# Attention block with routed experts: the last batch from its last projection to the routed rows in two halves of two tiles

## The chip, the cores and the metric

One core of a Trainium2 chip. The metric is the device time of the whole program in microseconds, the median of the runs; lower is better. Engines are called by their short names: PE (TensorE, matmuls), DVE (VectorE), ACT (ScalarE), POOL (GpSimd) and SP (SyncE, which issues DMAs here). Each runs its own queue in order and waits on semaphores.

## The reference

Four batches of 512 tokens with 256 features pass through one block.

```python
mod = (silu(c) @ wmod).reshape(4, 6, 1, -1)          # sa, ca, ga, sb, cb, gb
ga = sign(ga) * max(abs(ga), 0.25);  gb likewise
h = layernorm(x) * (1 + ca) + sa
x = x + ga * attention(h)       # 16 heads of 128, rms norm of q and k, rope factors,
                                # scores capped by 50 tanh(s / 50), causal softmax, @ wo.T
h = layernorm(x) * (1 + cb) + sb
x = x + gb * (experts(h) + shared(h))
# experts: logits = h @ gate.T; softmax over 64; the best 3 of 8 groups, of these the best 6 experts;
# each token goes to slot flat * 96 + min(pos, 95); per expert silu(g) * u, times Wd; the six results
# are weighted and summed.  shared: silu(h @ Sg.T) * (h @ Su.T) @ Sd.T, width 352
```

Routing is sequential in the tokens: `pos`, the place of a token in its expert's buffer, counts all tokens before it.

## The kernel before

A batch is four tiles of 128 tokens (`TT` = 4). The attention runs in periods, one per head: in period `p` PE does the scores of head `p`, the transposes and the projection of head `p - 1`, the projections q, k, v of head `p + 2`, and the product of head `p`. The routing of batch `b` is laid over periods 1 to 15 of batch `b + 1`, a piece per period, and its 24 table writes (one indirect DMA for each tile and each of the six choices, `table`, L510 to L514) over periods 9 to 15 of POOL, as `SPREAD` says (L64). The last batch has no such cover. In its place stands the shared expert: `shared_up(j)` (L1391) is one third of a batch's first layer, so there are twelve, j = 0 to 11; ACT takes silu (`shared_silu`), DVE multiplies (`shared_mul`), PE multiplies by the second layer after every third (`shared_down(b)`, L1460), and DVE adds that to x (`shared_half`, `shared_res`). After that PE goes through the 64 experts.

The order of all this is written out by hand, engine by engine. For the last batch it reads, after the last period:

- PE (L1456 to L1497): `o_t` transposes the last head's output; `proj` multiplies it by the head's rows of `wo`; `shared_up(2)` and `(3)`; `h2_t` transposes the normed rows; half of `shared_down(0)`; `router` gives the logits; the other half; `shared_up(4)`; `positions`, which adds up the chosen experts over the tokens; `shared_up(5)`, `(6)`, `shared_down(1)`; a transpose of `lastp`, the last token of each expert; the rest of the shared work.
- DVE (L1145 to L1185): `wo_low`, `out_low` (the low part of the split operands), `x_most` adds fifteen heads, times the gate, to x; `x_last` does so with the last head; `ln_stats`, `h2_scaled`, `h2_modulated` make the normed rows in `pay`; then `route_soft`, `route_groups`, `route_experts`, `route_counts`, `route_slots`, and for each tile `route_tile`, after which POOL may write that tile's six tables.
- ACT (L707 to L717): the high parts of the operands, silu of groups 0 to 3, `h2_static` (copy of the transposed rows), `route_exp`, silu of the rest.
- POOL (L551 to L562): `ln_rstd`, the tables of tiles 0 and 1, the gather of the last tokens' rows (it needs `lastp`), the tables of tiles 2 and 3.
- SP (L410 to L431): weights of experts, the normed rows to memory, and, when all table writes have landed, the rows of the first eight experts.

PSUM has eight banks. Banks 0 to 3 hold the shared expert's first layer, 4 and 5 the projection (`yps`) and later `shared_down`; 6 and 7 the last batch's transposed rows, and 6 its logits and positions (`sbank`, L324).

Of the kernel before, what the change touches and what calls it, by code (L numbers as in the profile page):

```python
# [28 lines left out]
P = 128  # L29
# [11 lines left out]
C = 96  # L41
# [22 lines left out]
SPREAD = {9: (0, 3), 10: (3, 4), 11: (7, 4), 12: (11, 1), 13: (12, 4), 14: (16, 4), 15: (20, 4)}  # L64


def build(nc, x, wqkv, wo, qkw, cossin, ct, wmod, gate, sgu, sd, wgu, wd, out):
    with ExitStack() as ctx:
# [175 lines left out]
        def wd_place(v):  # L244
# [27 lines left out]
            wcol_rdy x_shared o95_g cmb_ps cmb cmb2 outd""".split()  # L272
# [6 lines left out]
        acc2_in = [sem(f"acc2_in{b}") for b in range(B)]  # L279
# [43 lines left out]

        def sbank(b):  # L324

            return 6 if is_last(b) else SB
# [3 lines left out]
        def _(sp):  # L330
# [86 lines left out]
            sp.wait_ge(s["h2s_rdy"], B)  # L417
# [19 lines left out]
            def third_sum():  # L437

                sp.wait_ge(ys[2], adds(2, E))
                for b in range(B):  # L440
                    sp.dma_start(accs[2][:, b * TT:(b + 1) * TT], acc_d[2][b * T:(b + 1) * T].rearrange("(i p) d -> p i d", p=P)).then_inc(acc2_in[b], 16)
# [21 lines left out]
        def _(pool):  # L463
# [22 lines left out]
            def ln_rstd(l):  # L486

                pool.wait_ge(s["aggr"], TT * (l + 1))
                pool.tensor_scalar(rstd[:], mv[:, :, 1], 1e-5, None, ALU.add).then_inc(s["var_eps"], 1)
                pool.wait_ge(s["var_eps"], l + 1)  # L490
                pool.tensor_tensor(rstd[:], rstd[:], neghalf[:, 0:TT], ALU.pow).then_inc(s["rstd_rdy"], 1)

# [58 lines left out]
            ln_rstd(ln2(B - 1))  # L551
            for i in range(TT // 2):
# [7 lines left out]
            for i in range(TT // 2, TT):  # L560
# [15 lines left out]
        def _(a):  # L576
# [49 lines left out]

            def wo_high(b, n):

                if some(cnt(b, n - 1)):
                    a.wait_ge(s["y_rdy"], 2 * cnt(b, n - 1))  # L630
                act_(woh[:], wos[:, bass.ds(head(n), 1), :].squeeze(1), ACT.Copy).then_inc(s["woh_rdy"], 1)
# [10 lines left out]
            def h2_static(b):  # L642

                a.wait_ge(s["xt_ps"], ln2(b) + 1)
                act_(h2s, ps[:, sbank(b):sbank(b) + KC, :], ACT.Copy).then_inc(s["h2s_rdy"], 1)

            def route_exp(b):

                a.wait_ge(s["soft"], b + 1)
                for i in range(TT):  # L650
                    ins = act_(lg[:, i, :], ps[:, sbank(b), i * E:(i + 1) * E], ACT.Exp, bias=mx[:, i:i + 1], accum_out=rs[:, i:i + 1])
# [131 lines left out]
        def _(v):  # L783
# [92 lines left out]

            def wo_low(b, n):
# [37 lines left out]

            def e3(ap, n):
                return ap.unsqueeze(2).to_broadcast([P, TT, n])

            def max8(b, v8, src, keep):

                for i in range(TT):
                    step(b, nc.vector.max(v8[:, i, :], src[:, i, :]), i == TT - 1)
                step(b, nc.vector.memset(v8[:, :, keep:8], -1.0))

            def taken(b, c, out, v8, src):

                for i in range(TT):
                    step(b, nc.vector.match_replace(out[:, i, :], v8[:, i, :], src[:, i, :], -1.0), i == TT - 1)

            def route_soft(b):  # L930
                rt[0] = 0
                v.wait_ge(s["logit_ps"], b + 1)
                nc.vector.tensor_reduce(mx, ps[:, sbank(b), 0:TT * E].rearrange("p (i e) -> p i e", i=TT), X, ALU.max, negate=True).then_inc(s["soft"], 1)

            def route_groups(b):

                v.wait_ge(s["rt_exp"], b + 1)
                step(b, nc.vector.tensor_reduce(gsc.rearrange("p i n -> p (i n)"), lg.rearrange("p i (n c) -> p (i n) c", n=NG), X, ALU.max))
                step(b, nc.vector.reciprocal(rs, rs), False)
                max8(b, g8, gsc, TG)  # L940
                taken(b, 4, gm, g8, gsc)
                step(b, nc.vector.scalar_tensor_tensor(out=tmp.rearrange("p i (n c) -> p (i n) c", n=NG),
                                                       in0=gm.rearrange("p i n -> p (i n)").unsqueeze(2).to_broadcast([P, TT * NG, GS]), scalar=0.0,
                                                       in1=lg.rearrange("p i (n c) -> p (i n) c", n=NG), op0=ALU.is_lt, op1=ALU.mult))

            def route_experts(b):

                max8(b, w8, tmp, K)
                taken(b, 5, left, w8, tmp)
                ts(selr[:], left, 0.0, None, ALU.is_lt).then_inc(s["sel_rdy"], 1)  # L950

            def route_counts(b):

                for i in range(TT):
                    step(b, nc.vector.max_index(ei[:, i, :], w8[:, i, :], tmp[:, i, :]), i == TT - 1)
                step(b, cp(pay[:, :, D + K:TOK], ei[:, :, 0:K]))
                step(b, tt(pay[:, :, D:D + K], w8[:, :, 0:K], e3(rs, K), ALU.mult), False)
                step(b, cp(pay[:, :, TOK].bitcast(I32), iotat[:, bass.ds(b * TT, TT)]), False)

            def route_slots(b):  # L960

                v.wait_ge(s["sel_rdy"], b + 1)
                v.wait_ge(s["pos_rdy"], b + 1)
                posv = ps[:, sbank(b), 0:TT * E].rearrange("p (i e) -> p i e", e=E)
                step(b, ts(over, posv, float(C - 1), SKIP, ALU.is_ge, ALU.mult))
                tt(slotm, posv, iota96[:].unsqueeze(1).to_broadcast([P, TT, E]), ALU.add).then_inc(s["pos_used"], 1)
                v.wait_ge(s["pos_used"], b + 1)
                step(b, tt(slotm, over, slotm, ALU.add))
# [17 lines left out]
            def route_last(b):  # L986
# [4 lines left out]
                step(b, nc.vector.tensor_reduce(count, sel.rearrange("p i e -> p e i"), X, ALU.add))  # L991
                step(b, tt(carr[:], carr[:].bitcast(F32), count, ALU.add))
# [12 lines left out]
            def rows_clamped():  # L1005
# [5 lines left out]
                                               op0=ALU.add, op1=ALU.mult).then_inc(s["mrow_rdy"], 1)  # L1011

            def period(b, p):
# [35 lines left out]
                if not (is_last(b) and isinstance(p, int) and p >= H - 2):  # L1049
                    squares_sum(b, p + 2)  # L1050
                if some(cnt(b, p - 1)):
                    y_add(b, p - 1)
                o_norm(b, p)
                if is_last(b) and isinstance(p, int) and p == H - 1:
                    shared_mul(0)
# [53 lines left out]
            def x_most(b):  # L1109

                v.wait_ge(s["y_added"], 2 * cnt(b, H - 2))
                xb = xs[:, b * TT:(b + 1) * TT, :]
                v.wait_ge(s["rows_in"], 16 * (b + 2))
                tt(yacc, yacc, rcur[:, 0:1, :].to_broadcast([P, TT, D]), ALU.mult).then_inc(s["x2_rdy"], 1)
                v.wait_ge(s["x2_rdy"], 2 * b + 1)
# [482 lines left out]
```

## Time and profile before

| what | us |
|---|---|
| median of 3 runs | 1039.97 |
| lowest, highest | 1035.8, 1043.36 |
| profiled execution, its own time | 1048.57 |
| its span, first to last instruction | 1046.7 |
| PE busy in the span | 982.6 (94%) |
| DVE busy | 680.4 (65%) |
| ACT busy | 586.1 (56%) |
| POOL busy | 382.6 (37%) |

The time line of the page cuts the span in 40 slices; a digit is the busy share in tenths.

```profile
PE   4999999999999999999999999999989789999992
PEld 4799999999999999999999999999955356566661
DVE  3566657768778876868887696788568133222366
ACT  2566766676666667666766666666541024433430
POOL 2222222223223554312354532235523615455660
PEclk9899999999999999999999999999999899999985
DMA  9992000001000101100010011100361049999747
```

One slice is 26 us. Attention fills the first 29 slices, up to about 770 us; the last batch's routing and the shared expert lie in slices 30 to 32, the experts from there to about 1010 us, and the rest adds the sums to x and writes it out. PEclk is the clock that PE was granted, in tenths of full speed: the higher of two levels, 2.4 GHz, is full, the lower is 1.2 GHz.

### The profile page before, as it was taken

How to read it: one execution, taken by the hardware profiler on the slowest of the kernel's cores; microseconds unless marked ns; L12 is line 12 of the kernel's file. 1: busy time of each engine (PE TensorE's matmuls, PEld its weight loads, DVE VectorE, ACT ScalarE, POOL GpSimd, SP SyncE). 2: the span in 40 equal slices, each digit the busy share in tenths (PEclk: the TensorE clock that was granted, in tenths of full speed). 3: DMA queues.
4: the chain of work that ended last, by engine and by line, in shares of the span. 5: the costliest groups of instructions: out<-in, count | busy, mean ns of one | idle time of the engine just before them, and what ended most of it. 6: DMA issues, size and time to landing. Idle time of an engine off the chain costs nothing.

```text
span 1046.7 us, 18148 instructions
## 1 busy us (share of the span) xinstructions
PE 982.6 (94%) x6301; PEld 874.1 (84%) x6301; DVE 680.4 (65%) x1775; ACT 586.1 (56%) x1093; POOL 382.6 (37%) x454
## 2 busy tenths in 40 slices
PE   4999999999999999999999999999989789999992
PEld 4799999999999999999999999999955356566661
DVE  3566657768778876868887696788568133222366
ACT  2566766676666667666766666666541024433430
POOL 2222222223223554312354532235523615455660
PEclk9899999999999999999999999999999899999985
DMA  9992000001000101100010011100361049999747
GB/s 348 335 348 90 0 0 1 1 2 56 2 1 18 43 33 38 36 22 1 13 46 28 24 37 60 49 3 15 99 180 57 17 118 303 300 292 298 164 74 240
DMA packets 67037, 99.22 MB, mean 95 GB/s; under 512 B 10157, under 2 KB 48176, under 8 KB 66574
## 3 DMA queue, kind: packets, MB, share of 16 engines
q1 hardware_dynamic: 41678, 70.43, 20.8%
q0 software_dynamic: 11808, 12.87, 6.2%
q10 hardware_dynamic: 13472, 14.90, 4.9%
q8 instruction: 46, 0.75, 0.3%
q14 instruction: 33, 0.27, 0.1%
HBM read 66.03 MB, written 38.78 MB: 100 GB/s over the span
## 4 chain that ended last, share of the span: by engine, by line
PE 79%; DVE 12%; issue 3%; ACT 2%; DMA 2%; POOL 1%; SPq 0%; POOLq 0%; DVEq 0%
PE ps L1308 22%; PE ps L1361 12%; PE ps L1334 11%; PE ps L1349 7%; PE ps L1514 7%; PE ps L1529 5%; PE ps L1398 3%; PE ps L1341 2%; PE ps L1317 2%; PE ps L1320 2%; PE ps L1507 1%; PE ps L1467 1%; PE ps L1521 1%; ACT prob L615 1%; DVE arena L975 1%
## 5 line engine op out<-in xcount | busy, mean ns | idle before, releaser
L615 ACT ACTIVATE prob<-ps,rn 128x512 f32<-128x512 f32 (+3 forms) x256 | 121.1, 526 | 122.3 <-PE ps L1334 115.4
L1308 PE MATMUL ps<-wh,hth 128*128 128x384 f32 x512 | 178.6, 349 | 5.7 <-DVE htl L814 3.6
L1308 PE MATMUL ps<-wh,htl 128*128 128x384 f32 x512 | 173.0, 338 | 0.0
L1308 PE MATMUL ps<-wl,hth 128*128 128x384 f32 x512 | 172.9, 338 | 0.0
L859 DVE TENSOR_REDUCE ss<-arena 128x8 f32<-128x1024 f32 x64 | 78.0, 1219 | 128.0 <-ACT arena L591 127.8
L1361 PE MATMUL ps<-vx,prob 128*128 128x129 f32 (+1 forms) x1280 | 153.4, 274 | 0.2 <-POOL prob L507 0.2
L1361 PEld LDWEIGHTS ps<-vx,prob 128*128 128x128 f32 x1280 | 148.2, 191 | 0.5 <-POOL prob L507 0.5
L591 ACT ACTIVATE arena<-ps 128x1024 f32<-128x1024 f32 x64 | 65.7, 1026 | 123.2 <-PE ps L1308 123.2
L504 POOL TENSOR_SCALAR_AFFINE_SELECT prob<-prob 128x384 f32<-128x384 f32 x64 | 35.4, 554 | 256.4 <-ACT prob L621 256.4
L570 POOL DMA_INDIRECT acc<-wos,arena x64 | 94.0, 1468 | 92.9 <-ACT wos L735 68.9
L513 POOL DMA_INDIRECT slot_rows<-pay,arena x96 | 99.4, 1035 | 43.2 <-issue 24.7
L498 POOL TENSOR_TENSOR rn<-rtmp,neghalf 128x8 f32<-128x8 f32 x64 | 105.3, 1645 | 5.3
L1308 PEld LDWEIGHTS ps<-wh,hth 128*128 128x128 f32 x512 | 97.6, 191 | 7.1 <-DVE htl L814 4.0
L1308 PEld LDWEIGHTS ps<-wl,hth 128*128 128x128 f32 x512 | 97.6, 191 | 0.0
L1308 PEld LDWEIGHTS ps<-wh,htl 128*128 128x128 f32 x512 | 97.2, 190 | 0.0
L1334 PE MATMUL ps<-qth,kth 128*128 128x512 f32 (+3 forms) x256 | 87.7, 342 | 6.4 <-DVE arena L889 4.0
L496 POOL TENSOR_SCALAR rtmp<-ss 128x8 f32<-128x8 f32 x64 | 12.5, 195 | 217.8 <-DVE ss L859 217.5
L1199 DVE TENSOR_TENSOR xn<-ps,arena 96x176 f32<-96x176 f32 x64 | 21.6, 337 | 104.0 <-ACT arena L726 80.5
L621 ACT ACTIVATE prob<-prob 128x1280 f32<-128x1280 f32 x64 | 83.7, 1308 | 0.0
L1334 PE MATMUL ps<-qtl,kth 128*128 128x512 f32 (+3 forms) x256 | 82.6, 323 | 0.0
L1334 PE MATMUL ps<-qth,ktl 128*128 128x512 f32 (+3 forms) x256 | 82.5, 322 | 0.0
L889 DVE TENSOR_TENSOR arena<-ps,arena 128x512 f32<-128x512 f32 x118 | 75.6, 681 | 3.5 <-PE ps L1349 3.4
(206 smaller groups left out, 2214.5 us busy)
## 6 DMA issues: line engine op xcount, KB each, us to landing
wge<-in_wgu SPq DMA_DIRECT2D x20, 352.0 KB
slot_rows<-pay SPq DMA_DIRECT2D x1, 6456.0 KB, 33.8
acc<-pay SPq DMA_DIRECT2D x3, 2048.0 KB, 18.1
arena<-slot_rows ACTq DMA_DIRECT2D x56, 100.9 KB
warena<-in_wqkv SPq DMA_DIRECT2D x1, 4992.0 KB, 20.8
arena<-in_wgu SPq DMA_DIRECT2D x14, 352.0 KB
warena<-acc SPq DMA_DIRECT2D x8, 512.0 KB, 6.9
late_t<-in_wd ACTq DMA_DIRECT2D x14, 192.0 KB
```

The source lines that it names most:

```text
L498: pool.tensor_tensor(rn[:, bass.ds(head(n), 1), :].squeeze(1), rtmp[:], neghalf[:], ALU.pow).then_inc(s["r_rdy"], 1)
L513: pool.indirect_dma_start(buf_d, bass.IndirectOffsetOnAxis(ap=sloti[:, i * K + k:i * K + k + 1], axis=0), pay[:, i, :], None, bounds_check ...
L570: pool.indirect_dma_start(acc_d[acc_of(e)], bass.IndirectOffsetOnAxis(ap=tokc[:, e % TR:e % TR + 1], axis=0), orow[e % ORING], None, bound ...
L615: act_(prob[:, OFF[j]:OFF[j] + w], sflat[:, OFF[j]:OFF[j] + w], ACT.Tanh, scale=rn[:, bass.ds(head(n), 1), TT + j:TT + j + 1].squeeze(1)). ...
L621: act_(prob[:, 0:1280], prob[:, 0:1280], ACT.Exp, scale=CAP).then_inc(s["expd"], 1)
L859: nc.vector.tensor_reduce(ss[:].rearrange("p (c i) -> p i c", c=2), sq, X, ALU.add).then_inc(s["ss_rdy"], 1)
L889: tt(ya, yp, ya, ALU.add).then_inc(s["y_added"], 1)
L1308: last = mm(ps[:, i, 0:3 * DH], hp[:, k, i * P:(i + 1) * P], wp[:, k, :], start=(k == 0 and m == 0), stop=(k == KC - 1 and m == 2))
L1334: last = mm(sflat[:, OFF[j]:OFF[j] + w], kp[:, j * P:(j + 1) * P], qp[:, T - w:T], start=(m == 0), stop=(m == 2))
L1349: last = mm(yps[:, i, :], op[:, i * P:(i + 1) * P], wp[:], start=(m == 0), stop=(m == 2))
L1361: last = mm(o, prob[:, c:c + P], vx[:, bass.ds((vslot(n) * TT + j) * (DH + 1), DH + 1)], start=(j == 0), stop=(j == i))
L1514: last = mm(ps[0:C, 1 + e % 2, 0:2 * M], xgt[:, e % 2, k, :], wgus[e % RING][:, k, :], start=(k == 0), stop=(k == KC - 1))
```

## The change

From the last head's projection on, the last batch's chain is cut into two halves of two tiles (`TH` = 2).

- The gate row is multiplied into the last head's rows of `wo` once, at period 12 (`wo_gate`), so the last projection comes out gated, and `x_last(q)` is one addition from PSUM. The sum of the other heads is gated inside the last period (`y_gated`).
- Transposed output, low parts, projection, x, statistics, rstd, modulation, transposes, copy, logits, exps and each routing step exist once for each half. The counts of the second half's positions include the first half's chosen experts.
- Banks: the halves of the last output go to 7 and 6, the transposed rows to 6 and 7, logits and positions of half q to bank 4 + q, `shared_down` to 6 and 7.
- PE's order: half of `shared_up(2)` stands before the last projection, half after it; `shared_up(3)` between the halves' routers; `shared_down(0)` in one piece after the first half's positions.
- POOL: three tiles' tables before the gather, one after it; `SPREAD` moves two writes from period 15 to period 12.
- The last batch no longer adds its counts to `carr`; the final loads of two accumulators use one semaphore with the third and wait until the third is scaled (`cmb2`).

```diff
-SPREAD = {9: (0, 3), 10: (3, 4), 11: (7, 4), 12: (11, 1), 13: (12, 4), 14: (16, 4), 15: (20, 4)}
+SPREAD = {9: (0, 3), 10: (3, 4), 11: (7, 4), 12: (11, 3), 13: (14, 4), 14: (18, 4), 15: (22, 2)}
+TH = TT // 2
...
+            sp.wait_ge(s["cmb2"], B)
             for a in range(2):
                 sp.wait_ge(ys[a], adds(a, E))
...
-            ln_rstd(ln2(B - 1))
-            for i in range(TT // 2):
+            ln_rstd_half(0)
+            ln_rstd_half(1)
+            for i in range(TT - 1):
...
-            out_t(B - 1, H - 1)
+            out_t_half(0)
+            out_t_half(1)
             shared_silu(2)
-            shared_silu(3)
             act_(warm[:], neghalf[:, 0:1], ACT.Exp)
-            h2_static(B - 1)
-            route_exp(B - 1)
-            for j in range(4, 3 * B):
+            h2_half(0)
+            route_exp_half(0)
+            h2_half(1)
+            route_exp_half(1)
+            for j in range(3, 3 * B):
...
+            def x_last(q):
+
+                v.wait_ge(s["y_rdy"], 2 * cnt(B - 1, H - 1) + (q - 1))
+                v.wait_ge(s["x2_rdy"], 2 * B + q)
+                xb = xs[:, (B - 1) * TT + q * TH:(B - 1) * TT + (q + 1) * TH, :]
+                tt(xb, xb, yps[:, q * TH:(q + 1) * TH, :], ALU.add).then_inc(s["y_added"], 1)
...
+            shared_mul(0)
+            x_most(0)
+            out_low_half(0)
+            out_low_half(1)
+            x_most(1)
+            x_last(0)
+            last_stats(0)
+            last_scaled(0)
+            x_last(1)
+            last_modulated(0)
             shared_mul(1)
...
+            route_slots(b, HALF[1])
+            route_tile(b, 2)
+            route_tile(b, 3)
             shared_half(0, 0)
...
+            shared_half(0, 1)
             shared_mul(5)
...
+            shared_up(2, (0,))
+            pe.wait_ge(s["y_added"], 2 * cnt(B - 1, H - 2))
+            pe.wait_ge(s["wol_rdy"], B * H)
+            last_proj(0)
+            last_proj(1)
+            shared_up(2, (1,))
+            h2_t_half(0)
+            router_half(0)
             shared_up(3)
...
+            h2_t_half(1)
+            router_half(1)
+            shared_up(4)
+            positions_half(0)
             pe.wait_ge(s["ld_sd"], 32)
...
+            shared_down(0)
             shared_up(5)
+            positions_half(1)
             shared_up(6)
             shared_down(1)
+            shared_up(7)
```

PE's queue before, from the end of the last projection to the second `shared_down` (L1398 is `shared_up`, L1467 `shared_down`, L1289 the transposes of the normed rows, L1378 the router, L1384 to L1387 the positions):

```order
L1398 MATMUL ps<-warena 96x512 x4
L1398 MATMUL ps<-warena 128x512 x4
L1289 MATMUL ps<-ident,pay 128x128 x8
L1467 MATMUL ps<-wos,warena 128x256 x6
L1378 MATMUL ps<-gates,arena 128x64 x8
L1467 MATMUL ps<-wos,warena 128x256 x6
L1398 MATMUL ps<-warena 128x512 x4
L1384 MATMUL ps<-selr,trir 128x256
```

The same place in the changed kernel (L1524 is `shared_up`, L1495 the transposes of a half, L1502 the router of a half, L1509 the first matmul of a half's positions):

```order
L1524 MATMUL ps<-warena 96x512 x2
L1495 MATMUL ps<-ident,pay 128x128 x4
L1502 MATMUL ps<-gates,arena 128x64 x4
L1524 MATMUL ps<-warena 128x512 x4
L1495 MATMUL ps<-ident,pay 128x128 x4
L1502 MATMUL ps<-gates,arena 128x64 x4
L1524 MATMUL ps<-warena 128x512 x4
L1509 MATMUL ps<-selr,trir 128x128
```

Ahead of the transposes stand two matmuls of `shared_up` where eight stood, and between transposes and router nothing where six of `shared_down` stood.

DVE's queue before, around the tiles of the routing (L978 ends a tile, L906 is `shared_mul`, here j = 5, L1132 and L1138 are `shared_half` and `shared_res`):

```order
L978 CAST arena<-arena 128x6
L906 TENSOR_TENSOR warena<-ps,warena 96x512
L1132 TENSOR_TENSOR warena<-ps,rgb 128x512
L1138 TENSOR_TENSOR xs<-xs,warena 128x1024
L975 SCALAR_TENSOR_TENSOR arena<-iotae,pay,arena 128x64 x6
```

In the changed kernel (L1021 to L1024 are `route_slots` of the second half, L1031 and L1034 a tile, L1218 `shared_half`, L943 `shared_mul`):

```order
L1021 TENSOR_SCALAR arena<-ps 128x128
L1022 TENSOR_TENSOR arena<-ps,iota 128x128
L1024 TENSOR_TENSOR arena<-arena 128x128
L1031 SCALAR_TENSOR_TENSOR arena<-iotae,pay,arena 128x64 x6
L1034 CAST arena<-arena 128x6
L1031 SCALAR_TENSOR_TENSOR arena<-iotae,pay,arena 128x64 x6
L1034 CAST arena<-arena 128x6
L1218 TENSOR_TENSOR warena<-ps,rgb 128x512 x2
L943 TENSOR_TENSOR warena<-ps,warena 96x512
```

`shared_mul(5)`, which stood after the second tile, now stands after the fourth and after both halves of `shared_down(0)`.

## Rows read from the trace of the kernel before

**Rows 1.** Windows: stretch, us, busy and count by engine, PEclk, DMA share, GB/s.
```profile
770.00:785.00 15.00, 12.32 (x42) 7.12 (x43) 12.34 (x25) 4.25 (x6) 1.64 (x2) 0.89 0.72 211
```

**Rows 2.** Timeline of PE: start, us, instruction, [idle before <-releaser].
```profile
765.13 2.40 PE L1361 MATMUL ps<-vx,prob 128*128 128x129 f32 x20
769.22 0.66 PE L1341 MATMUL ps<-ident,arena 128*128 128x128 f32 x4 [1.69 <-DVE arena L897]
771.67 0.36 PE L1349 MATMUL ps<-woh,oth 128*128 128x256 f32 x1 [1.79 <-DVE otl L875]
...
773.69 8.14 PE L1398 MATMUL ps<-warena 128*96 128x512 f32 x16
782.84 1.06 PE L1289 MATMUL ps<-ident,pay 128*128 128x128 f32 x8 [1.01 <-DVE pay L844]
```

**Rows 3.** Timeline of DVE, the hand-over.
```profile
770.88 0.69 DVE L875 TENSOR_TENSOR otl<-ps,oth 128x512 fp32r<-128x512 f32 x1 [0.78 <-ACT oth L625]
771.49 1.22 DVE L1114 TENSOR_TENSOR arena<-arena,rcur 128x1024 f32<-128x1024 f32 x1
...
774.48 1.21 DVE L1123 TENSOR_TENSOR arena<-ps,rcur 128x1024 f32<-128x1024 f32 x1
...
776.99 1.41 DVE L789 BATCH_NORM_STATS2 bst<-xs 128x6 f32<-128x256 f32 x4
...
781.04 1.66 DVE L844 SCALAR_TENSOR_TENSOR pay<-xn,rstd,rcur 128x256 f32<-128x256 f32 x4
```

**Rows 4.** Timeline of POOL, last LayerNorm and table writes.
```profile
778.90 0.51 POOL L489 TENSOR_SCALAR rstd<-mv 128x4 f32<-128x4 f32 x1 [9.60 <-DVE mv L792]
779.50 1.13 POOL L491 TENSOR_TENSOR rstd<-rstd,neghalf 128x4 f32<-128x4 f32 x1
799.12 1.09 POOL L513 DMA_INDIRECT slot_rows<-pay,arena  x1 [18.50 <-DVE arena L978]
...
815.52 1.00 POOL L558 DMA_INDIRECT lrow<-h_rows,lidx  x1 [0.30 <-issue]
...
830.92 0.97 POOL L513 DMA_INDIRECT slot_rows<-pay,arena  x1 [0.30 <-issue]
```

**Rows 5.** Timeline of PE, routing and shared matmuls.
```profile
798.98 3.70 PE L1398 MATMUL ps<-warena 128*128 128x512 f32 x8 [0.39 <-DVE warena L906]
...
808.43 0.30 PE L1488 MATMUL ps<-ident,arena 128*64 128x128 f32 x1 [0.56 <-DVE arena L990]
808.57 10.47 PE L1398 MATMUL ps<-warena 128*128 128x512 f32 x24
...
824.28 1.88 PE L1398 MATMUL ps<-warena 128*128 128x512 f32 x4
...
835.90 6.07 PE L1398 MATMUL ps<-warena 128*96 128x512 f32 x8 [1.10 <-issue]
843.38 5.46 PE L1467 MATMUL ps<-wos,warena 128*128 128x256 f32 x24 [1.41 <-DVE warena L906]
849.63 0.39 PE L1507 MATMUL ps<-ident,arena 96*128 96x96 f32 x2 [0.79 <-DVE warena L1132]
```

**Rows 6.** Timeline of ACT: copy of the transposed rows; silu of group 9.
```profile
783.94 1.02 ACT L645 ACTIVATE arena<-ps 128x1024 f32<-128x1024 f32 x1
...
832.40 0.60 ACT L705 ACTIVATE warena<-ps 128x512 f32<-128x512 f32 x1 [14.20 <-remote]
```

**Rows 7.** Lines of DVE, 785 to 812, by form: busy us, mean ns.
```profile
L975 DVE SCALAR_TENSOR_TENSOR arena<-iotae,pay,arena 128x64 f32<-128x64 f32 x24 | 5.3, 282 | 0.0
L1132 DVE TENSOR_TENSOR warena<-ps,rgb 128x512 f32<-128x512 f32 x4 | 2.7, 685 | 3.2 <-PE ps L1467 3.2
```

**Rows 8.** Timeline of SP: first rows of experts; first final load.
```profile
833.03 0.28 SPq L429 DMA_DIRECT2D arena<-slot_rows  x1
...
1020.82 0.36 SPq L454 DMA_DIRECT2D warena<-acc  x1
```

**Rows 9.** Timeline of DVE: scaling of the third sum's last quarter.
```profile
1014.20 1.21 DVE L1214 TENSOR_TENSOR warena<-warena,rgb 128x1024 f32<-128x1024 f32 x1
```

More of the change, by code:

```diff
@@ L914, in step @@
                     v.wait_ge(s["rt"], STEPS * b + rt[0])
+            ALL = (0, TT)
+            HALF = [(q * TH, (q + 1) * TH) for q in range(2)]
             def e3(ap, n):
[L917 to L928, printed above, removed]
@@ L946, in route_experts @@
[L946 to L958, printed above, removed]
@@ L960, in route_slots @@
[L960 to L968, printed above, removed]
+                return ap.unsqueeze(2).to_broadcast([P, ap.shape[1], n])
@@ new lines, in routed, with nth, max8 @@
+            def routed(b, r, c):
+                bank = 4 + r[0] // TH if is_last(b) else SB
+                n = r[1] - r[0]
+                return ps[:, bank, c * n * E:(c + 1) * n * E].rearrange("p (i e) -> p i e", e=E)
+            def nth(b, r):
+                return b + 1 + r[0] // TH
+            def max8(b, v8, src, keep, r):
+                for i in range(*r):
+                    step(b, nc.vector.max(v8[:, i, :], src[:, i, :]), i == r[1] - 1)
+                step(b, nc.vector.memset(v8[:, r[0]:r[1], keep:8], -1.0))
@@ new lines, in route_experts, with route_counts @@
+            def route_experts(b, r=ALL):
+                sl = slice(*r)
+                max8(b, w8, tmp, K, r)
+                taken(b, left, w8, tmp, r)
+                ts(selr[:, sl, :], left[:, sl, :], 0.0, None, ALU.is_lt).then_inc(s["sel_rdy"], 1)
+            def route_counts(b, r=ALL):
+                sl = slice(*r)
+                for i in range(*r):
+                    step(b, nc.vector.max_index(ei[:, i, :], w8[:, i, :], tmp[:, i, :]), i == r[1] - 1)
+                step(b, cp(pay[:, sl, D + K:TOK], ei[:, sl, 0:K]))
+                step(b, tt(pay[:, sl, D:D + K], w8[:, sl, 0:K], e3(rs[:, sl], K), ALU.mult), False)
+                if r[0] == 0:
+                    step(b, cp(pay[:, :, TOK].bitcast(I32), iotat[:, bass.ds(b * TT, TT)]), False)
@@ new lines, in route_slots @@
+            def route_slots(b, r=ALL):
+                sl, n = slice(*r), r[1] - r[0]
+                v.wait_ge(s["sel_rdy"], nth(b, r))
+                v.wait_ge(s["pos_rdy"], nth(b, r))
+                posv = routed(b, r, 1 if is_last(b) else 0)
+                step(b, ts(over[:, sl, :], posv, float(C - 1), SKIP, ALU.is_ge, ALU.mult))
+                tt(slotm[:, sl, :], posv, iota96[:].unsqueeze(1).to_broadcast([P, n, E]), ALU.add).then_inc(s["pos_used"], 1)
+                v.wait_ge(s["pos_used"], nth(b, r))
+                step(b, tt(slotm[:, sl, :], over[:, sl, :], slotm[:, sl, :], ALU.add))
@@ L1371, in h2_t @@
                 pe.wait_ge(s["hmod"], 2 * b + 2)
[L1372 removed]
+                xn_t(pay, SB)
             def router(b):
@@ L1392, in shared_up @@
+            def shared_up(j, us=(0, 1)):
                 b, m = j // 3, j % 3
@@ new lines, in _ @@
+            pe.wait_ge(s["o_normed"], 2 * B * H)
+            for i in range(TT):
+                last = pe.transpose(ps[:, 7 - i // TH, i * P:(i + 1) * P], on[:, i, :], ident[:])
+            last.then_inc(s["ot_ps"], 1)
+            shared_up(2, (0,))
[6 more added lines that the diff above has]
+            router_half(0)
```

237 lines of the change are left out of this document (148 added, 89 removed).

## The prediction

> **What bounds the kernel now.** I read the page first, then its chain of waits, then the order of time around the change. TensorE (PE) is busy in nearly every slice and makes most of the chain, so a gain must shorten PE's path. The change touches one place: the stretch between the last head's attention and the first expert. In its first 15 us the clock is 0.89 [rows 1]. Three things are to be seen there.
>
> First, the hand-over. PE ends the last head's product at 767.5, waits 1.69 and 1.79 us for VectorE (DVE) and ScalarE (ACT), projects, then has two of the `shared_up` groups as cover, and still waits 1.01 us at 782.84 for the modulated rows [rows 2]. DVE is the reason: after the split of the last transpose it does a product of 1024 columns and an addition of the same size before it looks at the last projection, and the same pair after it [rows 3]. Second, routing on DVE, then 24 table writes on GpSimd (POOL) from 799.12, one in about 1.3 us, with a gather at 815.52 among them; the last starts at 830.92 [rows 4]. SyncE can fetch the experts' rows at 833.03 [rows 8]. Third, PE does shared matmuls all the while and reaches the first expert at 849.63 [rows 5]. Rows were fetched long before: from 833.03 on, so **PE's own queue, not the routed rows, is the path**.
>
> **The stall.** Group 10 of `shared_up` should take what the groups before it took: 24 matmuls in 10.47 us are three groups, 3.45 each. It starts at 824.28, group 11 not before 835.90, and the last `shared_down` at 843.38 [rows 5]. That is 19.1 us where two groups and the row's own wait of 1.41 are 8.3: **10.8 us too long**. ACT shows the same: the silu of group 9, whose matmuls are recorded as ended by 819.04, runs at 832.40, half a microsecond after POOL's last table write ends (831.9) [rows 4 to 6]. PE works without a gap until 824 and then trickles, as if completions were held back from about the gather on.
>
> **The change part by part, on PE's path.** Times of the new kernel are counted on the old one's axis from 769.22, where the last transposes start in both.
>
> *Taken away.* (a) The 1.79 us ahead of the last projection: half of group 2 now stands there (1.7 us of matmuls; transposes end at 769.85, the half at 771.6, the first half of `otl` is ready at about 771.2). (b) The slow clock: 0.89 over 15 us is 3.3 us at the lower of the two levels, 1.65 us lost [rows 1]; it began in the second of two gaps near each other, and one of them is now filled. (c) The 1.01 us before the transposes of the rows. (d) 0.39 ahead of group 6 and 0.56 ahead of the transpose of the last positions [rows 5]. Together 5.4.
>
> *Brought in.* (e) PE projects until 773.0, does the other half of group 2 until 774.7, and then has nothing until the first half of the rows. That half: the projection's first half ends at 772.5; `x_last` is one 512-column step, 0.7 [rows 7]; statistics half of 1.41, 0.7; aggregates 0.2; POOL's two steps 1.8 (from its start at 778.90 to 780.63, and 0.1 to be started); modulation half of 1.66, 0.83; 0.14 to PE: 776.9 [rows 3, 4]. PE waits 2.2. (f) ACT's copy of each half stood behind a `shared_down` half before; now the router half follows at once. The copy of 1024 columns took 1.02 [rows 6], one of 512 about 0.6: 0.65 twice, 1.3. (g) `shared_down(1)` waits for `shared_mul(5)`, which DVE now does behind four more steps. PE: 776.9, transposes, copy and router half 2.15, group 3 to 782.5, second half to 784.65, group 4 to 788.1, positions 788.55, `shared_down(0)` 5.3 to 793.85, group 5 to 797.3, positions 797.9, group 6 to 801.35. DVE: slots of the second half 0.95 from 797.95, two tiles of 1.5 each (six of L975 and a cast [rows 7]), two 512-column steps 1.3, the product 0.65: 803.85. PE waits 2.5. (h) Group 9 waits about 0.3 for `shared_mul(7)`, now behind `shared_add(1)` after a later transpose. Together 6.3, and three more small position matmuls, 0.1.
>
> So without the stall **PE's path is longer by 1.0 us**, not shorter. Gate folding removes two 1024-column steps of DVE behind the projection [rows 3] and adds one of 256 columns at period 12, where PE is the bound; it is already in (e). The moved tables (3, 4, 4, 2 in place of 1, 4, 4, 4 at periods 12 to 15) cost nothing: four in a period are hidden now by a period of about 11 us. The final loads now also wait for the third sum's scaling, which starts at 1014.20 and runs 1.22, while SyncE gets there at 1020.82 [rows 8, 9]: 5.4 us of cover. The weights 15 to 17 are asked for about 4 us earlier, with nobody waiting.
>
> *The stall again.* POOL: first tile's slots at 788.6 + 0.95 + 1.5 = 791.05, the first write 0.8 later, 791.9 in place of 799.12: 7.2 us earlier. The same 25 starts end at about 824.7 in place of 831.9 [rows 4]. By (g), PE ends `shared_down(2)` at about 825.4 and only then starts group 10. If the hold ends with POOL's last write, it ends before PE would trip over it, and all 10.8 go. If it doesn't depend on POOL, none goes. Those are the bounds; the nearest row, ACT's start 0.5 us after POOL's end, speaks for the first.
>
> **The sum.** Against the profiled execution (1048.57, of which 1046.7 are its span): 1048.57 - 10.8 + 1.0 = 1038.8. The three timed runs, 1035.8 to 1043.36 with a median of 1039.97, lie 5 to 13 us below the profiled one. Without its stall the profiled one would be 1037.8, inside them. So I take it that the timed median holds about 2.2 us of such a stall: 1039.97 - 2.2 + 1.0 = **1038.8**.
>
> A rule against halving is in the Trainium skill, "VectorE: DVE Perf Modes", on the errata mechanism: one large tile pays the memory latency once, many small ones pay it each time. The trace agrees: a 1024-column step takes 1.22 and one of 512 takes 0.69 [rows 3, 7], so a split costs about 0.16. Some twenty steps are split, 3 us more on DVE, of which only what stands in (g) reaches PE.
>
> **Rivals.**
> Main case, 0.42: as above, 1038.8, by itself 1035 to 1042.
> A, 0.20: the stall is as large in the timed runs, and they are quicker than the profiled one for another reason. For: it is in ACT's and PE's rows alike. Against: the profiled run is 8.6 above the median, and that is nearly its size. 1039.97 - 10.8 + 1.0 = 1030.2.
> B, 0.16: the timed runs have none of it, the change then only lengthens PE's path: 1041.0. The Trainium skill has such a mechanism, "NOTIFIC — the notification-queue block", section "Overflow: three behaviours, one of which stalls the engine": records of the profile that back up can throttle an engine. No run here shows it yet.
> C, 0.17, slower: the clock. It fell in the old kernel at the gap of 1.79 that followed one of 1.69 [rows 1, 2]. The new gaps of 2.2 with 0.65 behind a short transpose group, and of 2.5, are as large; if both bring a fall of the size seen, that is 2 x 1.65, and with the stall's share unchanged 1039.97 + 1.0 + 3.3 = 1044.3. It decides from a gap of about 1.8 us that has another near it; against it, the single 1.69 and 1.41 are not followed by one.
> D, 0.05: the halves wait on each other longer than I see, or the rows come after PE (about 829 against 839.8 by my count), 1046 and more.
>
> **The numbers.** Low 1029 takes in A, high 1045 takes in C. Less than 1% can't be told from no change here, that is 10.4 us, 1029.6 to 1050.4. Faster by over 1% is the lower part of A and a little luck with the first half, 0.12; slower by over 1% the tail of D, 0.04; within, 0.84.
>
> **What would show it.** (a) No idle time at the last projection, and a clock of 1.0 in the 15 us after 770; if it is below, C. (e) An idle time near 2.2 before the first transposes of four. (g) One near 2.5 at the second `shared_down`. POOL's first table write of the batch near 792. For the stall: group 10 as one block, ACT's silu of group 9 right after its matmuls, the first expert's transpose at 839 to 841. If the trickle is there again at full length, the sum against the profiled execution is wrong by up to 10.8 us; if the path is clean and the timed runs fall to 1030, the share of the stall in the median was wrong.

## The result

| | median, us | runs |
|---|---|---|
| before | 1037.87 | 20, 1035.8 to 1043.36 |
| changed | 1042.09 | 20, 1038.34 to 1045.69 |

Changed to before: 1.0036, 95% interval 1.0026 to 1.0046. The change makes the kernel **slower by 4 us**, where the forecast was 1.2 us faster (1038.8 against 1039.97). Two later groups of runs gave 1.0038 (1.0025 to 1.0050) and 1.0039 (1.0026 to 1.0053). The profiled execution of the changed kernel took 1043.18 us, 1041.4 of them its span.

### The profile page after: what moved, and what is told of

It is laid out like the page before. It is cut to its first block, busy times and chain, and to the rows that moved or that the text cites. A ratio compares the mean times of both kernels' runs of the same rounds, so it can differ in the third digit from the quotient of the medians.

```text
span 1041.4 us, 18174 instructions
## 1 busy us (share of the span) xinstructions
PE 977.2 (94%) x6304; PEld 873.3 (84%) x6304; DVE 681.2 (65%) x1788; ACT 587.0 (56%) x1095; POOL 384.2 (37%) x456
## 4 chain that ended last, share of the span: by engine, by line
PE 75%; DVE 11%; DMA 7%; ACT 3%; issue 3%; POOL 1%; SPq 0%; ACTq 0%; POOLq 0%; DVEq 0%
PE ps L1406 22%; PE ps L1459 12%; PE ps L1432 11%; PE ps L1447 7%; DMA acc<-wos,arena 6%; PE ps L1653 4%; PE ps L1524 3%; PE ps L1668 3%; PE ps L1415 2%; PE ps L1590 2%; PE ps L1418 2%; PE ps L1439 2%; ACT prob L621 1%; DMA warena<-in_wqkv 1%; DVE bst L816 1%
```

## The profile after

The timeline of PE in the changed kernel; its first row answers to the transposes of [rows 2], its last to the first expert's of [rows 5]. L1524 is `shared_up`, L1590 `shared_down`, L1495 the transposes of the rows, L1502 the router.

```profile
769.16 0.66 PE L1604 MATMUL ps<-ident,arena 128*128 128x128 f32 x4 [1.18 <-DVE arena L935]
769.76 1.96 PE L1524 MATMUL ps<-warena 128*96 128x512 f32 x4
...
776.86 0.66 PE L1495 MATMUL ps<-ident,pay 128*128 128x128 f32 x4 [2.01 <-DVE pay L1111]
778.20 1.10 PE L1502 MATMUL ps<-gates,arena 128*128 128x64 f32 x8 [0.69 <-ACT arena L670]
...
782.63 0.60 PE L1495 MATMUL ps<-ident,pay 128*128 128x128 f32 x4
783.91 1.10 PE L1502 MATMUL ps<-gates,arena 128*128 128x64 f32 x8 [0.69 <-ACT arena L670]
...
788.60 5.44 PE L1590 MATMUL ps<-wos,warena 128*128 128x256 f32 x24
...
803.93 6.97 PE L1590 MATMUL ps<-wos,warena 128*128 128x256 f32 x24 [2.47 <-DVE warena L943]
...
818.36 3.67 PE L1524 MATMUL ps<-warena 128*128 128x512 f32 x8 [0.47 <-DVE warena L943]
821.86 5.36 PE L1590 MATMUL ps<-wos,warena 128*128 128x256 f32 x24
827.06 7.03 PE L1524 MATMUL ps<-warena 128*128 128x512 f32 x16
835.49 5.46 PE L1590 MATMUL ps<-wos,warena 128*128 128x256 f32 x24 [1.41 <-DVE warena L943]
841.74 0.39 PE L1646 MATMUL ps<-ident,arena 96*128 96x96 f32 x2 [0.78 <-DVE warena L1218]
```

The waits stand where they were counted: none at the projection, 2.01 for the first half of the rows (2.2 forecast), 0.69 twice for ACT's copies (0.65), 2.47 at the second `shared_down` (2.5), 0.47 at group 9 (0.3). What was not in the sum is in the second column: the second `shared_down` takes 6.97 us, the first 5.44 and the third 5.36 for the same 24 matmuls. Groups 10 and 11 (of `shared_up`) are one block of 7.03 us, so this execution has no stall.

DVE, POOL, ACT and SyncE of the same execution, answering to [rows 3], [rows 4], [rows 6] and [rows 8]. The DVE row is the modulation of the first half:

```profile
775.92 0.88 DVE L1111 SCALAR_TENSOR_TENSOR pay<-xn,rstd,rcur 128x256 f32<-128x256 f32 x2 [0.19 <-DVE xs L1086]
```

```profile
792.17 1.06 POOL L518 DMA_INDIRECT slot_rows<-pay,arena  x1 [12.34 <-DVE arena L1034]
...
825.22 0.98 POOL L518 DMA_INDIRECT slot_rows<-pay,arena  x1 [0.30 <-issue]
```

```profile
822.06 0.60 ACT L730 ACTIVATE warena<-ps 128x512 f32<-128x512 f32 x1 [3.55 <-PE ps L1524]
```

```profile
827.33 0.28 SPq L425 DMA_DIRECT2D arena<-slot_rows  x1
```

The first half's rows leave DVE at 776.8, POOL's tables start at 792.17 (791.9 forecast) and end 5.7 us earlier than in [rows 4]; the silu of group 9 follows its matmuls; the rows are fetched 14 us before PE needs them. All this is early for nobody: PE's queue is the path.

The windows of the same execution. The columns are those of [rows 1]; the seventh, behind POOL's, is the granted clock.

```profile
770.00:785.00 15.00, 11.62 (x53) 6.76 (x52) 11.04 (x35) 4.48 (x11) 2.63 (x4) 1.00 0.72 213
...
801.00:811.00 10.00, 7.53 (x27) 5.93 (x26) 7.10 (x22) 0.60 (x1) 7.96 (x7) 0.83 0.03 2
```

At the hand-over the clock is 1.00 in this execution where it was 0.89 [rows 1] (two later profiles of the same kernel, below, have 0.89 again); behind the 2.47 us wait it is 0.83 over 10 us, 3.4 us at the lower level (1.2 GHz). That is where `shared_down` lost 1.5 to 1.6 us.

## The experiments

**Path** below is the time from the last head's transposes to the first expert's transpose, on PE, in one profiled execution: 849.63 - 769.22 - 10.8 = 69.6 before, 841.74 - 769.16 = 72.6 after. Ratios are to the kernel before in the same group of runs, which share a chip. The ratio is worked out from all runs and not from the two medians. There were three groups, with the kernel before at 1046.55, 1038.13 and 1037.79 us. The changed kernel itself was not run in group 1, so a forecast "below the changed kernel" can be read in groups 2 and 3 only.

| run | group | path | falls of the clock on it | median | ratio (95%) |
|---|---|---|---|---|---|
| e1_mul5_early | 1 | 76.0 | 1 | 1047.14 | 0.9998 (0.9978 to 1.0017) |
| e2_dummy | 1 | 79.0 | 2 | 1045.46 | 0.9984 (0.9968 to 1.0001) |
| e3_fill | 1 | 75.1 | 1 | 1043.05 | 0.9956 (0.9939 to 0.9973) |
| e4_all | 1 | 72.6 | 1 | 1038.35 | 0.9910 (0.9889 to 0.9931) |
| before_again | 2 | 69.4 | 1 | 1036.99 | one execution |
| after_again | 2 | 74.4 | 2 | 1042.28 | 1.0038 (1.0025 to 1.0050) |
| e6_gate | 2 | 68.8 | 1 | 1034.58 | 0.9972 (0.9957 to 0.9986) |
| e4_again | 2 | 64.5 | 0 | 1031.44 | 0.9935 (0.9912 to 0.9957) |
| f1_warm2 | 3 | 71.0 | 0 | 1038.33 | 1.0003 (0.9992 to 1.0015) |
| e1_again | 3 | 70.0 | 1 | 1037.23 | 0.9996 (0.9984 to 1.0008) |
| e3_again | 3 | 68.0 | 0 | 1036.21 | 0.9977 (0.9961 to 0.9993) |
| after_third | 3 | 74.4 | 2 | 1042.39 | 1.0039 (1.0026 to 1.0053) |

### The two kernels again

> The kernel before, once more, for its profile beside the others of this call. Theory 1 (the 10.8 us for which group 10 of shared_up trickled was a rare event): no such stretch, the first transpose of the experts starts at 838 to 839. Theory 2 (completions of TensorE are held back while POOL writes its tables, in many executions and by a length that varies): a stretch of 3 to 13 us between 800 and 832 in which group 8's or 9's silu starts late after its matmuls, ended within 3 us of POOL's last table write.

> The changed kernel, timed on the same chip as the experiments. Theory 1 (the change costs 3.7 us by TensorE's waits and clock, whatever the chip): 0.3 to 0.5% above the kernel before. Theory 2 (the held completions are part of the timed runs on a chip where the kernel before takes 1046 instead of 1038 us, and the change, which lets POOL start 7 us earlier, moves or loses them): the ratio differs from 1.0036, either 0.5% or more below 1 (the stall gone, as the forecast's case A had it) or above 1.006.

> The changed kernel, beside its three variants on one chip. Theory (TensorE's waits and the slow clock in them): 0.3 to 0.5% above the kernel before, with one or two falls of the clock between 775 and 812. Rival (if this is the chip of the first call, where late completions cost every kernel 7 to 9 us): within 0.2% of the kernel before.

PE of before_again, and its window over the hand-over:

```profile
773.51 8.74 PE L1398 MATMUL ps<-warena 128*96 128x512 f32 x16
782.17 1.06 PE L1289 MATMUL ps<-ident,pay 128*128 128x128 f32 x8
...
823.42 7.03 PE L1398 MATMUL ps<-warena 128*128 128x512 f32 x16
...
838.10 0.38 PE L1507 MATMUL ps<-ident,arena 96*128 96x96 f32 x2 [0.79 <-DVE warena L1132]
```

```profile
770.00:777.00 7.00, 6.18 (x17) 3.94 (x18) 6.77 (x9) 0.00 (x0) 0.00 (x0) 0.51 0.79 224
```

No stall, and the first transpose of the experts at 838.1, as theory 1 had it: group 10 is in one block, and the whole execution takes 1036.99. The clock falls at the hand-over, longer than in the first profile (0.51 over 7 us), and there it costs next to nothing: the slow matmuls end when the rows come, 782.2, and the wait of 1.01 [rows 2] is gone instead. The rows come 13.5 us after the last transposes where they came 13.6 us after them in the first profile.

The changed kernel's second profile:

```profile
776.05 0.66 PE L1495 MATMUL ps<-ident,pay 128*128 128x128 f32 x4 [2.00 <-DVE pay L1111]
777.39 1.10 PE L1502 MATMUL ps<-gates,arena 128*128 128x64 f32 x8 [0.69 <-ACT arena L670]
...
784.81 1.10 PE L1502 MATMUL ps<-gates,arena 128*128 128x64 f32 x8 [0.69 <-ACT arena L670]
...
804.81 7.14 PE L1590 MATMUL ps<-wos,warena 128*128 128x256 f32 x24 [2.46 <-DVE warena L943]
```

```profile
770.00:785.00 15.00, 11.62 (x45) 6.18 (x43) 10.24 (x33) 3.97 (x9) 2.63 (x4) 0.89 0.66 191
777.00:785.00 8.00, 6.92 (x22) 3.62 (x22) 4.37 (x19) 1.64 (x6) 1.31 (x2) 0.79 0.34 117
801.00:811.00 10.00, 7.54 (x25) 5.44 (x24) 7.95 (x29) 0.60 (x1) 7.87 (x8) 0.83 0.03 2
```

And the windows of its third profile, after_third:

```profile
777.00:785.00 8.00, 6.94 (x22) 3.43 (x20) 4.87 (x21) 1.64 (x6) 1.31 (x2) 0.79 0.38 131
801.00:811.00 10.00, 7.55 (x24) 5.26 (x23) 8.45 (x33) 0.60 (x1) 7.87 (x8) 0.83 0.03 2
```

The waits are the same to 0.01 us, but the clock fell **twice**. From one router half to the other it takes 7.42 us where the first profile has 5.71: 1.7 us for the fall at 777 to 785, which the first profile did not have. The third profile has both falls too. Over the 15 us from 770 on these two have 0.89, as much slow clock as the kernel before had [rows 1]: it only stands behind another wait. So the path is 74.4 in two of three, and against 69.5 before that is 4.9 us more, in the first 3.1; the medians differ by 4.2, 4.2 and 4.6.

### Throwaway work in the waits

e2_dummy:

```diff
             shared_up(6)
+            for _ in range(5):
+                mm(ps[:, 4, D:2 * D], ident[:], sds[:, 0, :], start=True, stop=True)
             shared_down(1)
```

> The changed kernel, with ten throwaway passes (five fp32 products of 128x128 by 128x256 of a constant, some 2.1 us) that TensorE does in its wait before the second round of down projections; nothing reads them. The wait itself stays. Theory (the clock fell because TensorE was idle for those 2.47 us, and shared_down(1) took 6.97 us instead of 5.4 for it): the granted clock stays at 1.0 in this stretch, shared_down(1) takes 5.4 us, and the time is 1.3 to 1.7 us below the changed kernel. Rival (the clock fell for another cause, such as what the chip as a whole drew, and only happened to fall there): the dip stays or moves, and the time is the same within 0.5 us, or 0.3 us longer.

Inconclusive: it fell in group 1. There every profile has a stretch of late completions, in which an instruction has ended by its record and what waits for it goes on only several us later (more of it in the last section). It made the wait at `shared_down(1)` 4.89 us behind the throwaway passes, and the clock fell in it. f1_warm2 has this edit and one at the other wait:

```diff
             shared_up(2, (1,))
+            for k in range(KC):
+                mm(ps[:, 7, :], sgus[:, k, 0, 0:P], h2t[:, 0, k, :], start=True, stop=True)
             h2_t_half(0)
```

> The changed kernel, with throwaway passes in two of TensorE's waits: two products of 128x128 by 128x512 (four passes, 1.8 us) ahead of the first transposes of the payload, where it waits 2.0 us, and the ten passes of e2_dummy (2.15 us) ahead of shared_down(1), where it waits 2.47. Nothing reads them, the waits stay. Theory (each of these gaps lets the granted clock fall to 0.5 in most executions, at 1.7 us of path each; both falls are seen in the second profile of the changed kernel, one in the first): no fall between 765 and 815, the time 1.7 to 3.4 us below the changed kernel and within 1.5 us of the kernel before. Rival (the clock falls by what the chip draws and not by TensorE's idle time): the falls stay, the time is the same as the changed kernel's within 0.5 us.

PE and the windows of f1_warm2:

```profile
775.81 0.66 PE L1495 MATMUL ps<-ident,pay 128*128 128x128 f32 x4 [0.30 <-DVE pay L1111]
...
802.85 5.46 PE L1590 MATMUL ps<-wos,warena 128*128 128x256 f32 x24 [0.28 <-DVE warena L943]
...
839.15 0.38 PE L1650 MATMUL ps<-ident,arena 96*128 96x96 f32 x2 [0.78 <-DVE warena L1218]
```

```profile
777.00:785.00 8.00, 7.16 (x31) 4.40 (x32) 4.94 (x25) 1.99 (x10) 1.31 (x2) 1.00 0.48 172
801.00:811.00 10.00, 9.72 (x39) 7.02 (x38) 6.13 (x12) 0.05 (x1) 7.87 (x8) 1.00 0.03 2
```

The useful work starts no earlier for the passes: the rows come 7.69 us after the last head's transposes, as in the changed kernel (7.70), and `shared_down(1)` 19.98 us after the second router half (20.02). But the clock stays at 1.00, `shared_down(1)` takes 5.46, and the median falls from 1042.39 to 1038.33. **Work whose result nobody reads saves 4.1 us**; nearly all of what the change cost is the clock. This is the run that decides: the rival (falls stay, no gain) is out, and the gain is even above the theory's 1.7 to 3.4. The path explains 3.4 of it; the other 0.7 is not explained.

### Taking the waits away

e1_mul5_early and e1_again are one kernel: DVE does what `shared_down(1)` waits for ahead of `route_tile` (the ranks) of tiles 2 and 3.

```diff
             route_slots(b, HALF[1])
-            route_tile(b, 2)
-            route_tile(b, 3)
             shared_half(0, 0)
             shared_half(0, 1)
             shared_mul(5)
+            route_tile(b, 2)
+            route_tile(b, 3)
```

> The changed kernel, with DVE's two shared_half of round 0 and the product of group 5 put ahead of the ranks of tiles 2 and 3 of the last batch. Theory 1 (the 2.47 us that TensorE waits before the second round of down projections, and the slow clock behind it, 1.6 us, are lost on the path of TensorE): both go, the first transpose of the experts starts 3.5 to 4.1 us earlier than in the changed kernel (841.74), and the time is 3 to 4.5 us below it, the same as before the change within 1 us. POOL's last table gets its slots about 5 us later, which the experts don't wait for as long as it is done before 838. Rival (the expert phase starts by what POOL and the gathers of the tables end, not by TensorE): no gain or a loss of 1 to 3 us, with the first transpose waiting for the gathered rows. Rival (the 3.7 us come from the landings of the scatter-adds in the expert phase): the first transpose is earlier and the end is not.

> The changed kernel with shared_half(0, 0), shared_half(0, 1) and shared_mul(5) ahead of the ranks of tiles 2 and 3, once more, since its first run met a stretch of 4 to 15 us in which completions came late. Theory (without that stretch the 2.47 us wait and the slow clock behind it both go): 3 to 4.5 us below the changed kernel, the second round of down projections without a wait. Rival (DVE's route_last, now 1.9 us later, makes TensorE wait for the transposition of the last ranks instead): 0 to 2 us below.

PE of e1_again:

```profile
775.04 0.66 PE L1495 MATMUL ps<-ident,pay 128*128 128x128 f32 x4 [2.01 <-DVE pay L1111]
...
801.18 5.36 PE L1590 MATMUL ps<-wos,warena 128*128 128x256 f32 x24
```

In group 1 its path met the late completions (DVE stood still for 4.2 us, PE waited 3.3 and 2.4 us further on), so only the second run decides between theory and rival. There the wait and the fall behind it are gone, and the median is 5.2 below the changed kernel, of which 4.1 were counted (2.47 + 1.6); the forecast had 3 to 4.5. The other wait, 2.01, still brings its fall. Nothing behind it grew: the ranks had slack.

e3_fill and e3_again are one kernel: halves of groups 3 and 4 go into the waits around transposes and router, and DVE does `shared_mul(1)` before `x_last(0)` and `shared_mul(2)` before `last_modulated(1)`.

```diff
             x_most(1)
+            shared_mul(1)
             x_last(0)
...
             last_modulated(0)
-            shared_mul(1)
             last_stats(1)
             last_scaled(1)
+            shared_mul(2)
             last_modulated(1)
             route_soft(b, HALF[0])
-            shared_mul(2)
...
             shared_up(2, (1,))
+            shared_up(3, (0,))
             h2_t_half(0)
+            shared_up(3, (1,))
             router_half(0)
-            shared_up(3)
             h2_t_half(1)
+            shared_up(4, (0,))
             router_half(1)
-            shared_up(4)
+            shared_up(4, (1,))
```

> The changed kernel, with halves of groups 3 and 4 of the shared expert's up projection put into the three waits of TensorE around the transposes and router of the last batch (2.01, 0.69 and 0.69 us), and the products of groups 1 and 2 each one step earlier on DVE. Theory (TensorE's own order is what these waits cost, and each comes off the end): 3.0 to 3.4 us of waits are filled, of which 0.6 comes back as DVE's product ahead of x_last(0) holds back the first rows by 0.6 us and some 0.3 at the next positions; the time is 1.5 to 2.5 us below the changed kernel. Rival (the waits only move to the next place where TensorE needs DVE, the positions of the first half or the second round of down projections, since DVE's chain is the longer one): the 2.47 us wait grows by 1.5 to 2.5 us and the time is the same within 0.7 us.

> The changed kernel with halves of groups 3 and 4 in TensorE's waits around the last batch's transposes and router, once more for the same reason. Theory (the waits and the slow clock at the first of them go, but DVE's chain then sets shared_down(1), which waits for the product of group 5): the wait at shared_down(1) is 4 to 5 us instead of 2.47, and the time is 0.5 to 2.5 us below the changed kernel, of which 0.8 to 1.7 is the clock that no longer falls at 777 to 782. Rival: the waits are filled for their full 3 us and the clock besides, 3.5 to 5 us below.

PE of e3_again, and its window:

```profile
776.18 0.66 PE L1495 MATMUL ps<-ident,pay 128*128 128x128 f32 x4 [0.28 <-DVE pay L1111]
...
800.19 5.46 PE L1590 MATMUL ps<-wos,warena 128*128 128x256 f32 x24 [2.56 <-DVE warena L943]
```

```profile
801.00:811.00 10.00, 10.00 (x36) 6.29 (x35) 5.10 (x13) 0.60 (x1) 7.87 (x8) 1.00 0.03 2
```

6.2 us below the changed kernel, more than the rival had (3.5 to 5). The wait at `shared_down(1)` did not grow (2.56). DVE's chain moved forward with PE's, since DVE had itself been waiting for PE: for the second half's logits 0.93 us where the changed kernel has 1.88, for the first half's positions nothing where it has 1.39. And here a wait of 2.56 us was **not** followed by a fall, with the hand-over's waits filled. So a wait of that length does not always bring one. In group 1 the wait was 7.23 us, by the late completions, and the clock did fall behind it.

e4_all and e4_again have both edits, and `shared_mul(7)` ahead of `shared_add(1)`.

> The changed kernel with both edits: products of group 5 and the two shared_half ahead of the ranks of tiles 2 and 3, the halves of groups 3 and 4 in TensorE's three waits, and DVE's product of group 7 ahead of the sum of the shared expert. Theory (both gaps lie on TensorE's path, and nothing else holds the expert phase): the first transpose of the experts starts at 834 to 836 instead of 841.7, the time is 5 to 7.5 us below the changed kernel and 1.5 to 4 us below the kernel before the change. Rival (POOL's table of tile 3 and the gathers behind it are then the bound, about 837): the first transpose waits for the gathered rows, and the time is 3 to 4.5 us below the changed kernel, no better than with the first edit alone.

> The changed kernel with both edits of before (products of group 5 and shared_half ahead of the ranks of tiles 2 and 3; halves of groups 3 and 4 in TensorE's three waits; product of group 7 ahead of the sum), once more beside the changed kernel. Theory (it wins by TensorE's waits filled and by nothing of that chip's state): again 0.7 to 1.0% below the kernel before, and 5 to 7.5 us below the changed kernel. Rival (its 0.9% came from where the held completions fell in that call): the ratio to the kernel before is within 0.4% of 1.

PE of e4_again:

```profile
775.75 0.66 PE L1495 MATMUL ps<-ident,pay 128*128 128x128 f32 x4 [0.28 <-DVE pay L1111]
...
832.52 0.39 PE L1648 MATMUL ps<-ident,arena 96*128 96x96 f32 x2 [0.78 <-DVE warena L1218]
```

In group 1 the first expert's transpose came at 841.2 and not at 834 to 836, by the late completions; in group 2 it came at 832.5, ahead of the forecast. The rival of e4_again (within 0.4% of the kernel before) is out, narrowly. **This version beats both kernels**: 1031.44, 0.9935 (0.9912 to 0.9957) of the kernel before and 10.8 us below the changed one, where 5 to 7.5 were forecast. Path 64.5: 8.1 below the changed kernel's with one fall, 9.9 below it with two. The halves are worth having once PE has work in the waits that they open.

### The gate alone

e6_gate is the kernel before with the gate folded in, half of group 2 ahead of the last projection, and `wo_low` moved into the last period, as in the changed kernel; nothing in halves of the batch. The core of its diff:

```diff
+                tt(wos[:, H - 1, :], wos[:, H - 1, :], rcur[:, 0, :], ALU.mult).then_inc(s["g_rdy"], 1)
...
-                tt(yacc, yps, rcur[:, 0:1, :].to_broadcast([P, TT, D]), ALU.mult).then_inc(s["y_added"], 2)
-                v.wait_ge(s["y_added"], 2 * cnt(b, H - 1))
-                tt(xb, xb, yacc, ALU.add).then_inc(s["x2_rdy"], 1)
+                tt(xb, xb, yps, ALU.add).then_inc(s["y_added"], 2)
...
             o_t(B - 1, H - 1)
+            shared_up(2, (0,))
```

> The kernel before with two parts of the change alone: the gate folded into the last head's weights and the rest of the sum, and half of group 2 of shared_up put ahead of the last projection. No halves of the batch, no banks moved, no router or ranks by halves. Theory (the hand-over was worth 4.45 us on TensorE's own order, of which 2.4 us can be had without the halves, as DVE's x_last loses one pass of 1024 elements (1.3 us) and the 1.8 us before the projection are filled): 1.5 to 3 us below the kernel before. Rival (the 1.0 us wait at h2_t grows by what is gained before it, since DVE's chain sets it): 0 to 1.3 us below.

PE of e6_gate, and its window:

```profile
779.92 1.40 PE L1301 MATMUL ps<-ident,pay 128*128 128x128 f32 x8 [2.04 <-DVE pay L846]
...
785.09 1.89 PE L1390 MATMUL ps<-gates,arena 128*128 128x64 f32 x16
```

```profile
777.00:785.00 8.00, 5.96 (x23) 4.49 (x22) 3.37 (x8) 3.11 (x4) 0.71 (x1) 0.79 0.76 264
```

1.5 to 4.5 us faster by the interval, which takes in the theory's 1.5 to 3. The rows come 2.3 us earlier than in before_again (11.17 against 13.47 us after the last transposes). In this execution a fall of the clock behind the 2.04 us wait takes 1.7 of it back (router at 785.09 against 785.67); the median suggests that many executions keep it, which one profile cannot show. The medians of this group are 1038.13 before, 1034.58 with the gate alone and 1031.44 with e4's order: of e4's 6.7 us some 3.5 are to be had without any halves, and the halves, with their fills and e4's order on DVE, add about 3.1.

## Why the prediction was wrong

**The step that failed is the sum: it credited the clock where it had been slow and did not charge it where the new waits stand.** Step (b) took off 1.65 us for the slow clock that the change removes, and the new gaps of 2.2 and 2.5 were charged their idle time only; their own falls were put off to rival C, with 0.17. They are the rule: the fall at the second `shared_down` is in 3 of 3 profiles of the changed kernel, the one behind the first rows in 2 of 3. (With e1 and e2, whose order is the same up to there, it is in 4 of 6.) C's price, 2 x 1.65, was right within 0.2 (1.7 and 1.5 to 1.7 measured). f1_warm2 shows the cause: no falls on the path, 4.1 us less.

**The second error is the base.** The step "the timed median holds about 2.2 us of such a stall" rested on a comparison of two times only, and no run bears it out. The median of the three runs shown, 1039.97, lay above that of 20 runs, 1037.87, and that is the profiled execution without its stall, 1037.8. So B's case fits the numbers (no stall in the timed runs, nothing to be given back), though no trace shows those runs. The forecast was 1.2 us faster, measured were 4.2 slower: of the 5.4 between them the falls are about 3.3 and the stall that was not there 2.2.

C holds beside B: 1037.87 + 1.0 + 3.3 = 1042.2, measured 1042.09. I had treated them as exclusive, and added C to a base 2.1 us too high. That the sum meets to 0.1 is partly luck: on the path the waits cost 0.4 to 0.6 more than 1.0, and one profile in three has a single fall.

Point by point:
- (a), (c), (d): gone as said. (b): the clock is 1.00 over the hand-over in one profile only; in the other two it is 0.89 over the same 15 us, as before, so what was credited came back. And in the old kernel the slow clock cost little there, as before_again shows: PE was waiting for DVE anyway.
- (e), (f), (g), (h): 2.01, 2 x 0.69, 2.47, 0.47 against 2.2, 2 x 0.65, 2.5, 0.3.
- The waits' balance, +1.0: f1_warm2, with the waits and without the falls, has a path of 71.0 against 69.4 and 69.6, so +1.4 to +1.6. The half microsecond over the forecast is most likely the splitting of PE's own work, which the sum left out: counted from their start to the next one, or to their end where PE then waits, the transposes take 0.66 + 0.60 in halves and 0.90 in one piece, the router 0.94 + 0.95 and 1.73, together 0.5. In the medians the balance is only +0.5 (1038.33 against 1037.79, ratio 0.9992 to 1.0015).
- POOL's first write, the rows, the final loads (the first starts at 1015.63, 5.3 us behind the end of the third sum's scaling): as forecast, and without effect. POOL's last write ends 5.7 us earlier, not 7.2.
- "If the hold ends with POOL's last write, all 10.8 go": not borne out where a stall occurred. e1_mul5_early lets POOL start at 791.8, and its time in group 1 was still the kernel before's (0.9998), as in group 3 (0.9996).

**What stays open.** From the first expert's transpose to the span's end the profiles have 195.5 to 201.6 us (197.1 twice before; 199.7, 201.6 and 198.7 changed; 195.5 and 199.8 for one and the same kernel). Whether a part of that is the change's can't be said from single executions; the path alone gives 3.1 to 4.9 us, with the measured difference between them. The clock also falls now and then among the experts: f1_warm2 has such a fall between 910 and 930 (0.90 and 0.93 over the two stretches of 10 us), e3_fill one between 920 and 930 (0.83). And what makes the clock fall at one wait of 2.0 us and not at another of the same kernel is not explained. The length of the wait alone does not decide: before_again has a fall behind 1.46 us that followed 1.18, and behind the 1.4 us ahead of the last `shared_down` no profile has one (5.46 us for its 24 matmuls each time).

## What to carry to other kernels

Charge a new wait on PE's path twice: its idle time, and the slow matmuls behind it, which here cost 1.5 to 1.7 us behind most waits of 2.0 to 2.5 us. When a chain is cut into halves to come earlier, PE's own queue must be cut as finely, so that a piece of independent work stands in the waits; then the halves paid (from 0.4% slower to 0.2% faster with the waits around the transposes filled, to 0.65% with both edits). Before a forecast is taken from a median of three, see whether the profiled execution without its one-off event agrees with it.

## What the runs showed of the hardware

**A stretch of late completions, in all profiles of one group of runs.** In group 1 all kernels were slower than in groups 2 and 3: the kernel before by 8.6 us, the version with all edits by 6.9 (1038.35 against 1031.44), e1 by 9.9, e3 by 6.8. The profiles of that group show where. In e4_all, PE, ACT and POOL:

```profile
802.77 3.60 PE L1524 MATMUL ps<-warena 128*128 128x512 f32 x8
811.22 0.42 PE L1631 MATMUL ps<-ident,arena 128*64 128x128 f32 x1 [4.84 <-DVE arena L1046]
```

```profile
814.23 0.60 ACT L730 ACTIVATE warena<-ps 128x512 f32<-128x512 f32 x1 [15.15 <-remote]
```

```profile
810.59 0.97 POOL L518 DMA_INDIRECT slot_rows<-pay,arena  x1 [0.30 <-issue]
```

Group 7's matmuls end at 806.4 and its silu starts at 814.2, with nothing else for ACT to do; DVE stands still from 800.7 to 805.6 in the same way. POOL writes the tables of three tiles up to 811.6, and the silu starts 2.7 us later; DVE had gone on 6 us before POOL's end and then stood once more, until 814.3; in e1_mul5_early the two are 814.7 and 817.5, again 2.8 apart, in the kernel before 0.5 [rows 4, 6]. It shows only in the stretch in which POOL writes the last batch's tables one behind the other; all four profiles of group 1 and the first of the kernel before have it, the other nine don't, though POOL writes there in the same way. It is tied to the table writes in time; no run took them away, so that they are the cause is not shown. The path of e4 in group 1 is 72.6, in group 2 64.5: 8.1 us, and the medians differ by 6.9, so there the stall is part of the timed runs, as rival A had it for the kernel before. The Trainium skill's "NOTIFIC — the notification-queue block", section "Overflow: three behaviours, one of which stalls the engine", says that a full queue of records can be set to stall the engine that makes them; no run here tells whether it is that.
